# Query features, second pass: split fp32r products for the projection, and both parts of the tops in one signed product

## The reference, cut to what matters

```
norm = 16 ** -0.25
xp   = einsum('bhnd,md->bhnm', q * norm, proj)         # the projection, 64 values per head and token
diag = sum(q ** 2) * 0.5 * norm * norm                 # per head and token
stab = max(xp over its 64 features)                    # "the top" of a head and token
qp   = exp(xp - diag - stab) + 1e-4                    # (times a factor that cancels)
```

## Time and profile before

| what | value |
|---|---|
| median of 3 runs | 795.13 (793.34 to 795.24) |
| the profiled execution | 794.28, span 792.5 |
| PE, matrix products | 731.3 busy, 92% |
| DVE | 618.3 busy, 78% |
| ACT | 470.0 busy, 59% |
| POOL | 372.2 busy, 47% |
| mean granted clock of PE | 0.965 of full speed |

### The profile page before, as it was taken

One profiled execution on the slowest core, in us unless ns is written; L12 is line 12 of the kernel. 1 busy time (PEld: TensorE's weight loads), 2 busy tenths in 40 slices (PEclk: granted clock), 3 DMA queues, 4 the chain that ended last, 5 costly groups with the idle time before them and its releaser, 6 DMA issues. The chain is left out here.

```text
span 792.5 us, 16189 instructions
## 1 busy us (share of the span) xinstructions
PE 731.3 (92%) x6012; PEld 597.2 (75%) x6012; DVE 618.3 (78%) x1298; ACT 470.0 (59%) x749; POOL 372.2 (47%) x358
## 2 busy tenths in 40 slices
PE   8999999999999999999999979985899999999950
PEld 7867768778778778778778658875788889998850
DVE  5877678888888888788788696888858777777683
ACT  4656747767867867857857734464145544455470
POOL 4364407517517517517617512501337666445663
PEclk9999999999999999999999999989699999999985
DMA  8100010011011011011011011150256664556593
GB/s 249 33 2 2 1 54 2 27 54 56 28 54 54 26 53 54 26 53 54 26 53 30 28 57 52 57 194 0 70 178 168 159 153 99 122 152 167 117 276 118
DMA packets 51184, 62.60 MB, mean 79 GB/s; under 512 B 9408, under 2 KB 44992, under 8 KB 51136
## 3 DMA queue, kind: packets, MB, share of 16 engines
q1 hardware_dynamic: 44016, 49.74, 19.3%
q0 software_dynamic: 6864, 12.19, 8.0%
q10 hardware_dynamic: 256, 0.03, 0.0%
HBM read 40.85 MB, written 21.10 MB: 78 GB/s over the span
## 5 line engine op out<-in xcount | busy, mean ns | idle before, releaser
L2157 PE MATMUL pF<-w,h 128*128 128x256 f32 x448 | 109.8, 386 | 0.0
L2157 PEld LDWEIGHTS pF<-w,h 128*128 128x128 f32 x448 | 80.7, 190 | 17.6 <-issue 8.6
L1128 POOL DMA_INDIRECT kp<-row_scratch,idx_g x32 | 42.4, 1325 | 76.7 <-DVE idx_g L1829 52.8
L893 ACT ACTIVATE h<-pX,b1cur 128x512 f32<-128x512 f32 x64 | 44.1, 691 | 55.9 <-DVE b1cur L1929 41.5
L982 POOL TENSOR_SCALAR ve<-mv 128x4 f32<-128x4 f32 x36 | 8.5, 237 | 141.4 <-DVE mv L1205 140.5
L2607 PE MATMUL pX<-w_lo,h_hi 128*128 128x256 f32 x256 | 73.9, 289 | 0.8 <-issue 0.8
L2607 PE MATMUL pX<-w_hi,h_lo 128*128 128x256 f32 x256 | 72.4, 283 | 0.0
L2607 PE MATMUL pX<-w_hi,h_hi 128*128 128x256 f32 x256 | 72.4, 283 | 0.0
L1136 POOL DMA_INDIRECT acc_scratch<-qp,idx_s x28 | 56.6, 2021 | 21.7 <-DVE qp L1866 16.8
L1887 DVE TENSOR_TENSOR h_lo<-h,h_hi 128x512 fp32r<-128x512 f32 x64 | 42.8, 690 | 25.9 <-ACT h_hi L885 25.9
L1305 DVE RECIPROCAL den<-den 128x512 f32<-128x512 f32 x14 | 46.9, 3348 | 7.4 <-ACT den L541 7.4
(11 more groups left out here) (434 smaller groups left out, 2171.9 us busy)
## 6 DMA issues: line engine op xcount, KB each, us to landing
kp<-fc1T SPq DMA_DIRECT2D x8, 1024.0 KB, 7.1
w<-fc2T SPq DMA_DIRECT2D x8, 1024.0 KB, 8.1
xin<-video SPq DMA_DIRECT2D x7, 512.0 KB, 3.8
x<-video SPq DMA_DIRECT2D x7, 512.0 KB, 4.5
out<-x SPq DMA_DIRECT2D x7, 512.0 KB, 3.0
acc_scratch<-xf SPq DMA_DIRECT2D x7, 512.0 KB, 2.9
row_scratch<-y SPq DMA_DIRECT2D x7, 512.0 KB, 3.0
kp<-acc_scratch SPq DMA_DIRECT2D x4, 512.0 KB, 5.7
```

What stands on the lines that cost most here:

```text
L893: nc.scalar.activation(h[:, n, :], pM[n % M_SLOTS], ACT.Gelu_apprx_tanh, bias=b1cur[:, n:n + 1]).then_inc(he_ready, 1)
L1128: pool.indirect_dma_start(xg[:, g, :], None, row_d, bass.IndirectOffsetOnAxis(ap=idx_g[:, g:g + 1], axis=0)).then_inc(gathered, 16)
L2157: ins = nc.tensor.matmul(pF[m][:, half * D:(half + 1) * D], h[:, k, tok(2 * m + half)], w2[:, k, :], start=(k == 0), stop=(k == FC - 1))
```

## The change

1. PE's `features_turned` replaces the one f32 product of the projection by three in fp32r: `projbd_lo` x `q_hi`, `projbd_hi` x `q_lo`, `projbd_hi` x `q_hi`. The first pass keeps its f32 products.
2. `q_hi` is a new copy by ACT (`q_high`), `q_lo` a new subtraction by DVE (`rest_of_queries`), placed ahead of `k_top` in the body and behind it in `first_batch`. `ql_ready` now counts 3 a batch (`L_STEPS`). Both tiles lie in the space of `qp`'s upper half.
3. The two products of the tops become one. `q_max` writes to a dense `mxq`; a new DVE copy (`both_tops`), behind `q_max` 3, writes each head's top to two rows of `mxp`, so that the transposed bank holds every top twice. `rest_of_tops` writes one tile, `mxT`: on the first four rows of each 32 the high part, on the next four the high part minus the exact top (`rest_rows` is -1 there and 0 elsewhere). The selector `selm` has -1 on the first four and +1 on the next four. `qmx_ready` now counts 5 a batch (`Q_STEPS`), and `turn_tops` waits for the fifth.
4. Constants for these are built by DVE ahead of the first batch. One semaphore of the later selection stage is merged into another.

The core of the diff (the declarations of tiles and semaphores and the changed counts in waits are left out):

```diff
+            def q_high(i):
+                act.wait_ge(qT_ready, (i + 1) * G)
+                nc.scalar.activation(q_hi[:], qT[:], ACT.Copy).then_inc(qh_ready, 1)
...
             def first_batch():      # ACT
                 q_squares(0)
+                q_high(0)
...
                 if is_ahead(i):     # ACT, body
+                    q_high(i)
                     values(i, 0)
...
                     queries(i, 0)
                     queries(i, 1)
+                    q_high(i)
                     values(i, 0)
...
+            def rest_of_queries(i):
+                dve.wait_ge(qh_ready, i + 1)
+                nc.vector.tensor_tensor(q_lo[:], qT[:], q_hi[:].bitcast(F32), ALU.subtract).then_inc(ql_ready, 1)
             def rest_of_tops(i):
                 dve.wait_ge(mxT_ready, i + 1)
-                nc.vector.tensor_tensor(mxT_lo[:], pXall[:, 0, :], mxT_hi[:].bitcast(F32), ALU.subtract).then_inc(ql_ready, 1)
+                nc.vector.scalar_tensor_tensor(out=mxT[:], in0=pXall[:, 0, :], scalar=rest_rows[:, 0:1], in1=mxT_hi[:].bitcast(F32),
+                                               op0=ALU.mult, op1=ALU.add).then_inc(ql_ready, 1)
+            def both_tops(i):
+                dve.wait_ge(qmx_ready, i * Q_STEPS + TT)
+                nc.vector.tensor_copy(mxp.rearrange("p t (a x r) -> p (t a) x r", a=4, r=4)[:, :, 0:2],
+                                      mxq.rearrange("p t (a r) -> p (t a) r", r=4).unsqueeze(2).to_broadcast([P, TT * 4, 2, 4])).then_inc(qmx_ready, 1)
...
                 k_top(0, sa)        # DVE, first_batch
+                rest_of_queries(0)
                 rest_of_squares(0)
...
                     q_max(i, 0)     # DVE, body
                     q_max(i, 1)
+                    rest_of_queries(i)
                     k_top(i, sa)
                     rest_of_squares(i)
...
                     q_max(i, 2)
                     q_max(i, 3)
+                    both_tops(i)
                     k_sub(i, 2)
...
-            nc.vector.tensor_scalar(selm..., of_head..., -1.0, None, ALU.mult)
+            built.link(nc.vector.tensor_reduce(of_rest[:], ident[:].rearrange("p (a r) -> p r a", a=4)[:, 4:8], AX_X, ALU.add))
+            built.link(nc.vector.tensor_reduce(rest_rows[:], of_rest[:], AX_X, ALU.add))
+            nc.vector.tensor_scalar(rest_rows[:], rest_rows[:], -1.0, None, ALU.mult)
+            built.link(nc.vector.tensor_tensor(of_head[:], of_rest[:], of_head[:], ALU.subtract))
+            nc.vector.tensor_copy(selm..., of_head...)
+            built.link(nc.vector.tensor_copy(projbd_hi[:], projbd[:]))
+            nc.vector.tensor_tensor(projbd_lo[:], projbd[:], projbd_hi[:].bitcast(F32), ALU.subtract)
...
                 def turn_tops():
                     slot_x(i, J_MT)
+                    pe.wait_ge(qmx_ready, (i + 1) * Q_STEPS)
...
-                    parts = ((projbd[:], qT[:, g, :]), (selc, qsq_hi[:, g, :]), (selc, qsq_lo[:, g, :]),
-                             (selm[:, g], mxT_hi[:]), (selm[:, g], mxT_lo[:]))
+                    parts = ((projbd_lo[:], q_hi[:, g, :]), (projbd_hi[:], q_lo[:, g, :]), (projbd_hi[:], q_hi[:, g, :]),
+                             (selc, qsq_hi[:, g, :]), (selc, qsq_lo[:, g, :]), (selm[:, g], mxT[:]))
```

More of the change, by code:

```diff
@@ L58 @@
 J_MH, J_MY = 0, 8
+Q_STEPS, L_STEPS = TT + 1, 3
 A_JOBS, X_JOBS, F_JOBS, U_JOBS = 19, 7, 12, 4
@@ L162, in build @@
         dgk = sb("dgk", [P, TT, H])
+        projbd_hi, projbd_lo = sb("projbd_hi", [P, 2 * M], F32R), sb("projbd_lo", [P, 2 * M], F32R)
         selc = sb("selc", [P, 2, M], F32R)
@@ L167, in build @@
         of_head = sb("of_head", [P, 4])
+        of_rest = sb("of_rest", [P, 4])
+        rest_rows = sb("rest_rows", [P, 1])
         epsmask = sb("epsmask", [P, 2])
@@ L181, in build @@
         qsq_lo = sb("qsq_lo", [P, G, N], F32R)
-        mxT_hi, mxT_lo = sb("mxT_hi", [P, N], F32R), sb("mxT_lo", [P, N], F32R)
+        mxT_hi, mxT = sb("mxT_hi", [P, N], F32R), sb("mxT", [P, N], F32R)
+        mxq = qe[:].rearrange("p a b -> p (a b)")[:, 2 * N:2 * N + TT * H].rearrange("p (t h) -> p t h", t=TT)
         mxp = qe[:].rearrange("p a b -> p (a b)")[:, (G + 1) * N:(G + 2) * N].rearrange("p (t x) -> p t x", t=TT)
+        with ExitStack() as before_qp:
+            before_qp.enter_context(nc.sbuf_tensor("q_raw", [P, PAIRS // 2, N], F32))
+            q_hi, q_lo = (before_qp.enter_context(nc.sbuf_tensor(n, [P, G, N], F32R)) for n in ("q_hi", "q_lo"))
         qp = sb("qp", [P, PAIRS, N])
@@ L327, in build @@
         sq_ready, dg_ready = sem("sq_ready"), sem("dg_ready")
+        qh_ready = sem("qh_ready")
         xk_ready, kmx_ready, kmax_ready, stab_ready = sem("xk_ready"), sem("kmx_ready"), sem("kmax_ready"), sem("stab_ready")
@@ L344, in build @@
         sel_const, s_turned, s_ready = sem("sel_const"), sem("s_turned"), sem("s_ready")
-        cnt_ready, sgn_ready, tot_ready, dve_s, vsum_ready, cand_ready = (
-            sem("cnt_ready"), sem("sgn_ready"), sem("tot_ready"), sem("dve_s"), sem("vsum_ready"), sem("cand_ready"))
+        cnt_ready, sgn_ready, tot_ready, vsum_ready, cand_ready = (
+            sem("cnt_ready"), sem("sgn_ready"), sem("tot_ready"), sem("vsum_ready"), sem("cand_ready"))
         pair_ready, off_ready, place_ready, place_turned = sem("pair_ready"), sem("off_ready"), sem("place_ready"), sem("place_turned")
@@ L603, in eps_k @@
                 nc.scalar.activation(kp[:, t, :], kp[:, t, :], ACT.Identity, bias=epsk_c[:, 0:1]).then_inc(kp_ready, 1)
+            def q_high(i):
+                act.wait_ge(qT_ready, (i + 1) * G)
+                nc.scalar.activation(q_hi[:], qT[:], ACT.Copy).then_inc(qh_ready, 1)
             def q_squares(i):
                 act.wait_ge(qT_ready, (i + 1) * G)
-                wait(act, ql_ready, i * 2)
+                wait(act, ql_ready, i * L_STEPS)
                 nc.scalar.activation(qsqT, qT[:], ACT.Square).then_inc(qsq_ready, 1)
@@ L1385, in first_batch @@
                 q_max(0, 3)
+                both_tops(0)
                 k_sub(0, 2)
@@ L1512, in _ @@
             nc.vector.tensor_scalar(selc[:], of_half[:].unsqueeze(2).to_broadcast([P, 2, M]), -0.5 * NORM * NORM, None, ALU.mult)
-            nc.vector.tensor_scalar(selm[:].rearrange("p g k m -> p (g k) m"), of_head[:].unsqueeze(2).to_broadcast([P, 2 * G, M]), -1.0, None, ALU.mult)
+            built.link(nc.vector.tensor_reduce(of_rest[:], ident[:].rearrange("p (a r) -> p r a", a=4)[:, 4:8], AX_X, ALU.add))
+            built.link(nc.vector.tensor_reduce(rest_rows[:], of_rest[:], AX_X, ALU.add))
+            nc.vector.tensor_scalar(rest_rows[:], rest_rows[:], -1.0, None, ALU.mult)
+            built.link(nc.vector.tensor_tensor(of_head[:], of_rest[:], of_head[:], ALU.subtract))
+            nc.vector.tensor_copy(selm[:].rearrange("p g k m -> p (g k) m"), of_head[:].unsqueeze(2).to_broadcast([P, 2 * G, M]))
+            built.link(nc.vector.tensor_copy(projbd_hi[:], projbd[:]))
+            nc.vector.tensor_tensor(projbd_lo[:], projbd[:], projbd_hi[:].bitcast(F32), ALU.subtract)
             built.link(nc.vector.tensor_scalar(epsmask[:], of_half[:], EPS_K, None, ALU.mult))
@@ L1518, in _ @@
             to.n = B * STEPS_N
-            done = Steps(dve, dve_s, 0, 0)
+            done = Steps(dve, dve_f, 0, 0)
+            done.n = (B - 1) * STEPS_F
             def selection_numbers():
@@ L2056, in slot_x @@
                 elif n <= J_MT:
-                    pe.wait_ge(qmx_ready, i * TT + 2 * (n - J_XQ))
+                    pe.wait_ge(qmx_ready, i * Q_STEPS + 2 * (n - J_XQ))
                 elif n == J_QT:
-                    pe.wait_ge(ql_ready, (i + 1) * 2)
+                    pe.wait_ge(ql_ready, (i + 1) * L_STEPS)
                 else:
@@ L2191, in features_turned @@
                         pe.wait_ge(qsq_ready, (i + 1) * 2)
-                    parts = ((projbd[:], qT[:, g, :]), (selc[:].rearrange("p k m -> p (k m)"), qsq_hi[:, g, :]),
+                    parts = ((projbd_lo[:], q_hi[:, g, :]), (projbd_hi[:], q_lo[:, g, :]), (projbd_hi[:], q_hi[:, g, :]), (selc[:].rearrange("p k m -> p (k m)"), qsq_hi[:, g, :]),
                              (selc[:].rearrange("p k m -> p (k m)"), qsq_lo[:, g, :]),
-                             (selm[:, g].rearrange("p k m -> p (k m)"), mxT_hi[:]), (selm[:, g].rearrange("p k m -> p (k m)"), mxT_lo[:]))
+                             (selm[:, g].rearrange("p k m -> p (k m)"), mxT[:]))
                     for n, (w_, x_) in enumerate(parts):
```

2 lines of the change are left out of this document (1 added, 1 removed).

## The result

The kernel after takes 801.05 at the median (799.53 to 801.53, 5 runs) where the kernel before takes 795.13 (792.36 to 795.85): a ratio of 1.0082, 95% interval 1.0068 to 1.0096. It is 5.9 slower; the forecast was 804.5 with a range of 794 to 809. The profiled execution has a span of 798.0 instead of 792.5.

A forecast was written before the change was run, and what follows sets the result against it. PE was taken to bound the kernel. Four loop batches at 1.57, two at 1.79, batch 1 at -0.73 and batch 0 at +0.25 gave +9.4 on 794.28, 803.7; adding 0.85 for the median, forecast 804.5, range 794 to 809.

The forecast's parts named there:

- `rest_of_queries` held by `xnb`: DVE's new subtraction waits for POOL's addition, ends 1.08 behind it, takes about 3.1 in the loop; `k_shift` 1.29 late.
- The rival in which it isn't held: `rest_of_queries` takes 1.2 beside POOL's `xnb`; -4.9 in all, 790.3; faster by either of two roads had chance 0.15.
- The stall for `sdiag`: PE's `spread_kmax`, which needs `sdiag` from DVE, moves from 258.90 to 259.41, a stall of 0.5 per loop batch.
- The second collision: POOL's first `ksum` addition gets in ahead of DVE's `k_sub(3)`, which loses 2.2; `features_turned(0)` 2.55 late, less 0.98 saved.
- The first rival: POOL doesn't get in before `k_sub(3)`, so only `turn_tops` is late: +3.3, 798.4; chance 0.25.
- `turn_tops` late: PE's `turn_tops` starts at 265.70, 1.54 late in all, with PE idle about 1.0 for `both_tops` in each loop batch.
- The saving of a call: Each PE call of `features_turned` falls from 2.00 to 1.51, saving 0.49, or 0.98 a batch and 7.8 over 16 calls.

The follow-up runs named there:

- e1: Kernel after, with POOL's addition `xnb` moved to the front of POOL's body from pass 1 on, every instruction kept: 788.06, ratio to before 0.9919.
- e2: Kernel before plus four unused tiles sized and placed like the new constants, shifting later tiles' addresses, no instruction changed: 789.63, ratio to before 0.9942.
- e3: Kernel after with only the split projection: no `both_tops`, two products for the tops as before: 796.2, ratio to before 1.003.
- e5: Kernel after with one more wait: POOL's `ksum` additions begin only when the batch's last `k_sub` is done: 794.14, ratio to before 1.0007.
- e11: Kernel before plus only the two small unused tiles, 4 words and 1 word a partition, without the two of 128 words: 789.37, ratio to before 0.9939.
- e9: Kernel after with `xnb` at the front of POOL's body and PE's `spread_kmax` ahead of half 1's first pass: 788.09, ratio to before 0.9934.
- e10: Kernel after with `xnb` and `spread_kmax` early, but batch 1's `xnb` back at its old place: 784.63, ratio to before 0.9882.
- e8: Kernel before with unused tiles at the new constants' places and `xnb` at the front of POOL's body, without the change: 791.64, ratio to before 0.9983.

## Why the prediction was right, and where it was not

Sign and mechanism held. The start of `features_turned(0)`, after less before, with what the terms of the prediction give at the same place (each batch's saving comes behind it):

| pass | 0 | 1 | 2 | 3 | 4 | 7 |
|---|---|---|---|---|---|---|
| before | 39.04 | 92.91 | 150.95 | 209.58 | 268.21 | 444.17 |
| after | 40.09 | 93.60 | 153.17 | 213.44 | 273.69 | 454.42 |
| later by | 1.05 | 0.69 | 2.22 | 3.86 | 5.48 | 10.25 |
| predicted | 0.75 | 0.50 | 2.29 | 3.86 | 5.43 | 10.36 |

- *`rest_of_queries` held by `xnb`*: its end 1.08 behind POOL's was the forecast to the hundredth, and the 3.2 for 3.1; e1 shows the cause. The rival in which it isn't held falls. e1, with `xnb` moved, is the kernel that this rival described, but it doesn't reach the rival's 4.9: at equal addresses it is 1.6 faster than before (e2), and its loop pass 0.52 shorter where the rival had 0.73.
- *The stall for `sdiag`*: 0.5 forecast, 0.50 measured.
- *The second collision*: POOL gets in ahead of the fourth `k_sub`, which ends 1.08 behind it; PE idles 0.99, and the way from `turn_tops` to `features_turned(0)` is 1.05 longer for 1.01 forecast. It was close: the forecast had POOL ready 0.3 ahead of that `k_sub`, and it was 0.13, with e3 on the other side of the boundary. The first rival (798.4) falls, and e5 puts the price at 6.0 to 6.9 where forecast and rival lay 6.1 apart. Here the Trainium skill, "SBUF — State Buffer", section on the two separate sides of SBUF, had the right outcome: the pair of ports goes whole to whoever starts first, and the other is blocked. The trace agrees in both directions, DVE blocked in the kernel after (4.52 for 2.35) and POOL in e3 (3.30 for 2.44).
- *`turn_tops` late*: the wait for `both_tops` was forecast at about 1.0 and is noted as 0.75. But an idle note isn't the whole price of a wait: from the start of the first pass of half 1 to `spread_kmax` PE took 1.00 before and 1.67 after (260.74 to 262.41), and the next product follows 0.32 behind instead of 0.22. So the noted 0.50 costs 0.77, the noted 0.75 moves `turn_tops` by 0.82, and together they make 1.59 for 1.54 forecast.
- *The saving of a call* was too high: 0.49 forecast, 0.40 measured. I priced six fp32r groups at 0.233 each. The first one, which follows work of another shape, takes 0.33 (273.69 to 274.02); the other five are 0.23. This is 0.18 a batch.
- *The addresses* were not in my sum at all. They make a loop pass 0.25 shorter (e2) and hide the misses above: against e2 the loop pass is 1.87 longer, where I had 1.57 (of the 0.30, 0.18 are the calls, 0.05 the two waits up to `turn_tops` and 0.04 the third). So it is luck, two errors that cancel, that forecast and measurement agree to about 0.1 in the table from pass 2 on: against e2 the last pass's call comes 12.44 later, not 10.36.

**Why 801.05 and not 804.5.** Up to the last pass the forecast is met, by the luck just told; the rest comes behind it, where the prediction changed nothing. The chain that ended last shows the 48 products of 128x512 at each start of an expert; of the kernel before, then of the kernel after:

```profile
570.79 11.21 PE pX L2094 x48
...
595.45 11.20 PE pX L2094 x48
```

```profile
578.44 10.92 PE pX L2134 x48
...
602.80 10.91 PE pX L2134 x48
```

The experts begin 7.65 later, so 2.6 is given back between the last pass (10.25) and there, 0.8 of it by that pass's two calls. The 8 experts then gain 0.29 each, 2.3, by the shorter products. Of the 1.8 that is left, a clock that stays up explains at least a part. Stretches of the kernel before (PEclk is the column behind the five engines' busy times):

```profile
440.00:473.50 33.50, 29.04 (x275) 19.72 (x274) 25.82 (x50) 19.07 (x27) 13.90 (x15) 1.00 0.14 48
473.50:477.00 3.50, 3.50 (x19) 3.50 (x18) 2.48 (x11) 1.28 (x3) 0.61 (x3) 0.51 0.55 150
```

and of the kernel after:

```profile
470.00:523.00 53.00, 45.82 (x324) 40.93 (x316) 44.12 (x135) 22.68 (x47) 18.64 (x36) 1.00 0.17 52
```

Before, PE idles 1.48 ahead of the last attention output and 2.02 ahead of the last batch's hidden products, and the granted clock falls to 1.2 GHz for 3.5; after, PE idles 1.46 and 2.04 at the same places, and there is no such stretch until 523. In e11, which has the tiles shifted and nothing else, the stretch is missing too, and from the last pass's first call to the experts it takes 125.19 (before 126.62, after 124.02); in e2 it is there, and it takes 126.30. So it comes and goes from version to version. What decides on it was not tried, and the idle doesn't tell them apart. The 0.3 by which pass 0 came later than forecast goes with the clock as well: from 31 to 38.5 it was 0.77 before and 0.54 after. e5, e9 and e10, with the same work in pass 0, had 0.77 and started the call at 39.50 to 39.79; e1 had 0.56 and started it at 40.58. That the clock is the cause of it was not tried.

## What to carry to other kernels

Before putting a VectorE subtraction with two SBUF inputs into a place, look at what POOL does there: beside a POOL addition it costs that addition's remaining time and its own, and delays of a few tenths can turn one collision into two. Move the POOL instruction, which nobody waited for, before judging the change: here the change made the kernel 1.4% slower (about 11) with POOL left alone, 0.2% faster with `xnb` moved (1.6, e1 beside e2) and 0.6% faster with two small moves more (4.7, e10 beside e11). Moving `xnb` was worth nothing without the change and cost 2 to 3 in batch 1 (e8); the move of `spread_kmax` was not tried without the change, where the loop has no idle for it to take away. When a change adds or removes tiles, time the old kernel with the new addresses as well.

## What the runs showed of the hardware that I had not expected

**A shift of tiles by 64 bytes changed the pace of the fp32r products of 128x512.** Groups of the kernel before and of e11, which differ by 5 unused words a partition (line, engine, operation, busy us and mean ns of one):

```profile
L2094 PE MATMUL pX<-x2T_hi,w_lo 128*128 128x512 f32 x128 | 50.7, 396 | 0.0
```

```profile
L2095 PE MATMUL pX<-x2T_hi,w_lo 128*128 128x512 f32 x128 | 50.0, 390 | 0.0
```

The chain of e11, beside the 11.20 of the kernel before:

```profile
591.91 10.91 PE pX L2095 x48
```

48 of them start 11.20 / 48 = 0.2334 apart before and 10.91 / 48 = 0.2273 apart in e11, e2 and every kernel with the change: 2.6%, at the same granted clock. The two tiles take 32 bytes each, so that everything behind them moves by 64; in the built programs `x2T_hi` lies at byte 138304 of a partition before, 64 past a multiple of 128, and at 138368 in e11 and 139392 in the kernel after, both multiples of 128. The weights of these products don't move: `w1_hi` lies at 32896 and `w1_lo` at 41088 in all of them, ahead of the unused tiles. The hidden products of the batches, with the same two weight tiles and `x2T`, are faster too, again before and e11:

```profile
L2094 PE MATMUL pF<-x2T_hi,w_hi 128*128 128x512 f32 x112 | 44.2, 395 | 0.0
```

```profile
L2095 PE MATMUL pF<-x2T_hi,w_hi 128*128 128x512 f32 x112 | 43.8, 391 | 0.0
```

So it is the place of the moving operand, or of what the other engines use meanwhile, not that of the weights. It isn't so for every fp32r product: in the experts' products of 128x256 weights (`h_hi`) and moving operand (`w2_hi`, `w2_lo`) both move by 64, and 48 of them take 5.75 before and after. No other distance than 64 and 1,088 was tried, so where the step lies stays open. In all, the 64 bytes are worth 4.2 to 4.6 (0.9942 and 0.9939): 2.3 in the experts and 1.4 between the calls of pass 0 and pass 7, the rest not assigned.

**POOL gets in between two DVE instructions that stand back to back**, if it starts 0.11 to 0.13 ahead of the start of the second (kernel after, all six passes from 2 to 7), and is itself stretched if it comes 0.12 to 0.15 behind it (e3, the same six passes).
